# Experts' second bias moved from TensorE to VectorE, and the next item's transposes dealt out among fc2's matmuls

## What is computed

```python
logits = cos_scores + route_scores
gates = _top_k_softmax(logits, TOP_K)                       # TOP_K = 2
h = gelu(einsum('bsd,edh->bseh', x, w1) + b1, approximate=False)
expert_out = einsum('bseh,ehd->bsed', h, w2) + b2           # w1 [8,1024,512], w2 [8,512,1024]
out = einsum('bse,bsed->bsd', gates, expert_out)
...
x = x + gb * out
```

## Time and profile before

| what | value |
|---|---|
| median of 3 runs | 1535.41 us (1529.23 to 1543.14) |
| the profiled execution's own time | 1545.17 us |
| its span, first to last instruction, slowest core (core 4) | 1543.6 us |
| spans of the eight cores | 1504.7 to 1543.6 us |
| PE busy over the span | 1184.6 us, 77% |
| DVE / ACT / POOL busy | 685.8 / 490.4 / 264.4 us |
| experts' stage | about 1265 to 1543.6 us |

### The profile page before, as it was taken

The page is one execution under the profiler, slowest core; times in us unless marked ns, Lnnn a source line. Parts: engine busy times, 40 slices in busy tenths (PEclk is TensorE's granted clock), DMA queues, the critical chain, the costliest instruction groups (busy, mean ns, idle before and its releaser), DMA issues.

```text
span 1543.6 us, 24787 instructions; the slowest of 8 cores (1504.7 to 1543.6 us)
## 1 busy us (share of the span) xinstructions
PE 1184.6 (77%) x8741; PEld 697.1 (45%) x8877; DVE 685.8 (44%) x1355; ACT 490.4 (32%) x1106; POOL 264.4 (17%) x364
## 2 busy tenths in 40 slices
PE   0317898848377887777998898999999705999996
PEld 0113444424234454444765565666666402343453
DVE  0266367636363566564242533525435331223332
ACT  0003455525244465422222232222332202332242
POOL 2022111100010000011012121212211120333333
PEclk9858999979698998667999999999999956999998
DMA  9953299999868567796953737558323396888865
GB/s 162 162 115 113 68 150 152 175 128 163 132 137 75 88 118 127 146 260 172 261 143 69 178 91 143 164 83 191 98 95 111 119 365 200 165 143 156 156 124 84
DMA packets 104448, 223.12 MB, mean 145 GB/s; under 512 B 14224, under 2 KB 47152, under 8 KB 100224
## 3 DMA queue, kind: packets, MB, share of 16 engines
q0 software_dynamic: 56240, 86.70, 38.7%
q1 hardware_dynamic: 28592, 107.77, 22.9%
q10 hardware_dynamic: 19488, 26.98, 9.8%
HBM read 192.64 MB, written 117.10 MB: 201 GB/s over the span
## 4 chain that ended last, share of the span: by engine, by line
PE 55%; DMA 15%; DVE 11%; issue 7%; ACT 4%; POOL 2%; another core or an unknown queue 2%; SPq 2%; ACTq 1%; POOLq 0%; DVEq 0%
PE bank L242 22%; PE pair L242 15%; PE bank L1057 11%; DMA y<-arena 5%; DMA arena<-s_x 3%; PE bank L250 3%; DMA arena<-wmod 3%; DVE arena L590 2%; DMA lnfm<-ln_fm 2%; SPq L235 2%; ACT arena L594 2%; DMA arena<-s_xsa 1%; PE pair L566 1%; PE pair L250 1%
## 5 line engine op out<-in xcount | busy, mean ns | idle before, releaser
L242 PE MATMUL bank<-arena 128*128 128x512 bf16 (+5 forms) x1648 | 369.5, 365 | 50.3 <-ACT arena L644 22.2
L242 PE MATMUL pair<-arena 128*128 128x256 bf16 (+3 forms) x2616 | 354.9, 281 | 17.6 <-DMA arena<-wqkvT 10.7
L242 PEld LDWEIGHTS pair<-arena 128*128 128x128 bf16 x2624 | 245.8, 99 | 119.3 <-issue 29.7
L1057 PE MATMUL bank<-arena 128*128 128x512 bf16 x960 | 255.6, 382 | 6.7 <-DVE arena L1076 3.1
L242 PEld LDWEIGHTS bank<-arena 128*128 128x128 bf16 (+2 forms) x1712 | 144.8, 101 | 220.3 <-issue 108.1
L1047 ACT ACTIVATE arena<-pair,fc1b_fm 128x256 bf16<-128x256 f32 x256 | 121.3, 474 | 352.9 <-PE pair L242 349.6
L594 ACT ACTIVATE arena<-pair,arena 128x384 bf16<-128x384 f32 x256 | 146.5, 578 | 173.1 <-DVE arena L590 146.1
L250 PE MATMUL bank<-ident_bf,arena 128*128 128x128 bf16 x1056 | 96.1, 239 | 76.0 <-DVE arena L468 36.3
L1401 DVE SCALAR_TENSOR_TENSOR arena<-bank,arena,repl 128x512 f32<-128x512 f32 (+1 forms) x96 | 71.9, 749 | 161.7 <-PE bank L242 161.7
L1057 PEld LDWEIGHTS bank<-arena 128*128 128x128 bf16 x1024 | 101.0, 99 | 75.4 <-issue 10.9
L250 PEld LDWEIGHTS bank<-ident_bf,arena 128*128 128x128 bf16 x1056 | 75.4, 107 | 110.8 <-issue 95.9
(11 more groups left out here) (144 smaller groups left out, 1032.7 us busy)
## 6 DMA issues: line engine op xcount, KB each, us to landing
arena<-s_w SPq DMA_DIRECT2D x32, 1024.0 KB, 22.4
arena<-x_ext SPq DMA_DIRECT2D x34, 512.0 KB, 6.2
s_w<-w_in POOLq DMA_DIRECT2D x16, 1024.0 KB, 12.9
s_xsa<-arena ACTq DMA_DIRECT2D x4, 2084.0 KB, 37.8
arena<-s_xsa ACTq DMA_DIRECT2D x32, 260.5 KB, 5.2
s_h<-arena SPq DMA_DIRECT2D x16, 512.0 KB, 4.4
arena<-wmod POOLq DMA_DIRECT2D x16, 512.0 KB, 11.1
arena<-s_h SPq DMA_DIRECT2D x16, 512.0 KB, 11.1
```

What stands on the lines that cost most here:

```text
L242: fn = (lambda e, l=l, r=r, i=i: e.matmul(out, l, r, start=(i == 0), stop=(i == n - 1)))
L1057: T_2[mu] = run("tensor", lambda e, lt=lt, n=n, b=b: e.matmul(bf(b)[:, :], tT[mu % 4][:, ts(lt, 128)], wf2[:, m, ts(n, 512)], start=(m == ...
```

## The change

The selector and its matmuls go. Each expert's b2 row is loaded to all 128 partitions (`rs(1)` and `rs(2)` in turn, a DMA of 512 KB issued by ACT), and DVE adds it in an operation of its own, out of PSUM into `yo`, before the product with gate and gb, which now reads and writes `yo` in SBUF. `turn(n)` returns its 8 transposes and its rest; `second_mm(n, beside)` puts one transpose behind each matmul, and the rest (copy, gate, place, load) comes behind the `second_mm` of the same index k.

```diff
-    sel_bf = A.alloc("sel_bf", [8, 8 * 128], BF16)
...
-    for e_ in range(NEXP):
-        c = ident_bf[0:8, e_:e_ + 1]
-        T_sel = run("vector", lambda e, e_=e_, c=c: e.tensor_copy(
-            sel_bf[0:8, ts(e_, 128)],
-            bass.AP(c.tensor, c.offset, [[c.ap[0][0], 8], [0, 128]])))
+    T_bb = {}
+
+    def load_b2(i):
+        T_bb[i] = move("scalar", rs(1 + i % 2), bass.AP(
+            b2_in.tensor, ITEMS[i][1] * D, [[0, 128], [1, D]]),
+            esem[f"bb{i % 2}"], T_fv.get(first.get(i - 1, 0) - 1))
+
+    load_b2(0)
+    load_b2(1)
...
     def turn(n):
 
         i, j, r0 = TILES[n]
-        T_xt[n] = transposes(bb(n % 2), xs[n % 8], 8, T_xsl[n], T_xe.get(n - 2))
...
+        def one(k):
+            fn = (lambda e: e.transpose(
+                bb(n % 2)[:, ts(k, 128)], xs[n % 8][:, ts(k, 128)],
+                ident_bf[:, :]))
+            if k < 7:
+                quiet("tensor", fn, T_xsl[n], T_xe.get(n - 2), T_id)
+            else:
+                T_xt[n] = run("tensor", fn)
+
+        def evac():
+            T_xe[n] = run("scalar", lambda e: e.activation(
+                xT3[:, :, ts(j, 128)], v3(bb(n % 2), 8), AF.Copy), T_xt[n],
+                T_f1.get((i - 1, 3)))
+            ex, s = ITEMS[i][1], n % 16
+            T_gate[n] = run("vector", lambda e: e.tensor_copy(
+                gate[:, s:s + 1], xtail[n % 8][:, 1 + ex:2 + ex]), T_xsl[n],
+                T_fv.get(n - 16))
+            T_place[n] = run("gpsimd", lambda e: e.tensor_copy(
+                place[:, s:s + 1], xtail[n % 8][:, 0:1]), T_xsl[n],
+                T_add.get(n - 16))
+            if n + 8 < len(TILES):
+                load_xs(n + 8)
+        return [lambda k=k: one(k) for k in range(8)], evac
...
-    def second_mm(n):
+    def second_mm(n, beside):
...
         for nn in range(2):
-            T_f2[n] = mms(bf(b + nn)[0:w, :],
-                          [(hT3[:, m, j * 128:j * 128 + w],
-                            w23[:, ex * 4 + m, ts(nn, 512)]) for m in range(4)]
-                          + [(sel_bf[0:8, ex * 128:ex * 128 + w],
-                              b2_bf[0:8, ts(nn, 512)])],
-                          T_fv.get(n - 2), T_g[4 * i + 3], T_e2[ex], T_sel)
-            T_fv[n] = run("vector", lambda e, nn=nn: e.scalar_tensor_tensor(
-                yo[n % 5][0:w, ts(nn, 512)], bf(b + nn)[0:w, :],
-                gate[0:w, s:s + 1], rs(0)[0:w, ts(nn, 512)], ALU.mult, ALU.mult),
-                T_f2[n], T_add.get(n - 5), T_gate[n], T_gb)
+            for m in range(4):
+                fn = (lambda e, nn=nn, m=m: e.matmul(
+                    bf(b + nn)[0:w, :], hT3[:, m, j * 128:j * 128 + w],
+                    w23[:, ex * 4 + m, ts(nn, 512)], start=(m == 0),
+                    stop=(m == 3)))
+                toks = (T_fv.get(n - 2), T_g[4 * i + 3], T_e2[ex])
+                if m < 3:
+                    quiet("tensor", fn, *toks)
+                else:
+                    T_f2[n] = run("tensor", fn)
+                for f in beside[:1]:
+                    f()
+                beside = beside[1:]
+            y, cols = yo[n % 5], slice(nn * 512, nn * 512 + 512)
+            tk = run("vector", lambda e, nn=nn, y=y, cols=cols: e.tensor_tensor(
+                y[0:w, cols], bf(b + nn)[0:w, :], rs(1 + i % 2)[0:w, cols],
+                ALU.add), T_f2[n], T_add.get(n - 5), T_bb[i])
+            T_fv[n] = run("vector", lambda e, y=y, cols=cols: e.scalar_tensor_tensor(
+                y[0:w, cols], y[0:w, cols], gate[0:w, s:s + 1],
+                rs(0)[0:w, cols], ALU.mult, ALU.mult), tk, T_gate[n], T_gb)
...
     for i in range(NI):
         for m in range(4):
             first_mm(i, m)
+            if m == 1 and 1 <= i < NI - 1:
+                load_b2(i + 1)
+        fs, evs = [], []
         for n in nxt.get(i + 1, ()):
-            turn(n)
-        for n in nxt[i]:
-            second_mm(n)
+            f, ev = turn(n)
+            fs += f
+            evs.append(ev)
+        for k, n in enumerate(nxt[i]):
+            second_mm(n, fs[8 * k:8 * k + 8])
+            if k < len(evs):
+                evs[k]()
```

More of the change, by code:

```diff
@@ L1249, in build_program @@
         [f"w1{i}" for i in range(8)] + [f"w2{i}" for i in range(8)]
-        + ["b1", "gb"] + [f"xs{i}" for i in range(8)]
+        + ["b1", "gb", "bb0", "bb1"] + [f"xs{i}" for i in range(8)]
         + [f"yo{i}" for i in range(5)])}
@@ L1359, in turn @@
         i, j, r0 = TILES[n]
-        T_xt[n] = transposes(bb(n % 2), xs[n % 8], 8, T_xsl[n], T_xe.get(n - 2))
-        T_xe[n] = run("scalar", lambda e: e.activation(
-            xT3[:, :, ts(j, 128)], v3(bb(n % 2), 8), AF.Copy), T_xt[n],
-            T_f1.get((i - 1, 3)))
-        ex, s = ITEMS[i][1], n % 16
-        T_gate[n] = run("vector", lambda e: e.tensor_copy(
-            gate[:, s:s + 1], xtail[n % 8][:, 1 + ex:2 + ex]), T_xsl[n],
-            T_fv.get(n - 16))
-        T_place[n] = run("gpsimd", lambda e: e.tensor_copy(
-            place[:, s:s + 1], xtail[n % 8][:, 0:1]), T_xsl[n], T_add.get(n - 16))
-        if n + 8 < len(TILES):
-            load_xs(n + 8)
+        def one(k):
[20 more added lines that the diff above has]
+        return [lambda k=k: one(k) for k in range(8)], evac
     def first_mm(i, m):
@@ L1419, in build_program @@
     for n in nxt[0]:
-        turn(n)
+        fs, ev = turn(n)
+        for f in fs:
+            f()
+        ev()
     for i in range(NI):
```

## The result

The changed kernel takes 1599.3 us (median of 4 runs, 1598.7 to 1600.1) beside 1535.4 us for the kernel before on the same chip (median of 3 runs, 1529.2 to 1543.1): ratio 1.041, 95% interval 1.035 to 1.047. A fourth run of the kernel before, at 1553.9 us, was in the slower state into which executions on all eight cores sometimes fall, and is left out. The change makes the kernel slower by 64 us. The prediction, 1582 us, had the sign, and 17 us too little of the size.

A forecast was written before the change was run, and what follows sets the result against it. PE was taken to bound the experts' stage. Held ACT queue and smaller terms gave +33.0, half clock 10.5 and 3, total +46.5: 1535.4 to 1582 us, forecast chance 0.51, range 1548 to 1604.

The forecast's parts named there:

- The wait that decides: ACT's next copy queues behind a load awaiting POOL's cast, behind DVE's scatter: large items 23.4 us against 20.56, +19.9 over seven.
- The port: POOL's casts may each sit out a DVE multiply with two SBUF inputs: up to 0.75 us each, 10 in all; taken 0.
- PE, what comes in: Moved transposes expose two PE waits in large items: 1.15 us between fc1 and fc2, 1.4 between fc2 and next fc1.
- A transposed pair at 0.27: On PE in fc2, a matmul plus a transpose takes 0.272 us, 2.18 for a tile's eight pairs; bounds 0.216 and 0.43.
- The clock: PE falls to half clock after gaps of about 4 us: 1.5 us per large item, 1.0 in items 8 to 10; +13.5.
- Item 8: First of the small items with ACT held until POOL's casts: +4.6 us, and 1.0 for half clock.
- The b2 loads at nothing: Loads of b2 rows hide on the DMA engines in large items; 0 to 2.9 us each in items 11 to 14, taken 0.
- Item 0's gain of 2.2: At the stage's start, item 0's transposes' stretch shrinks from 3.4 to 1.15 us: -2.2.
- rival B: DVE and POOL's shared port, or adds behind b2 loads in small items, add +10 to +20: 1592 to 1602 us; chance 0.15.
- A: Rival: ACT is held but PE's clock stays up: +33, 1568 us; chance 0.19.
- C: Rival: ACT isn't held; DVE through the banks and two exposed gaps remain, large items 19.6 us: -6, 1529; chance 0.10.
- D: Rival: ACT isn't held and DVE keeps up, PE's work and two gaps count: -19, 1516 us; chance 0.05.

The follow-up runs named there:

- experiment 1: The changed kernel with loads of xs tiles 8 and up issued by SyncE's queue instead of ACT's: ratio 1.016 to the kernel before, stage 266.8 us.
- experiment 2: The changed kernel with the next item's gate copies and casts ahead of all second_mm, copies and loads left in place: stage 261.5 us against the change's 308.4.
- experiment 6: The changed kernel with the bias back as an 8-row matmul and one DVE multiply, transposes still dealt among fc2's matmuls: stage 298.6 us, large items 24.0.
- experiment 8: The changed kernel with fc2's matmuls of small items' second tile on 128 columns of weights instead of 64: stage 300.7 us.
- experiment 7: The changed kernel plus 16 throwaway matmuls in PE's gap before fc1 in items 0 to 6: stage 296.4 us, large items 23.2 or 23.3, some 24.5.
- Experiment 10: The changed kernel without item 7's four scatters, their rows missing from the output: stage 301.5 us, item 8 15.1 to 15.2.
- experiment 5: The changed kernel without b2 loads for items 2 to 15, reusing the rows of items 0 and 1: ratio 1.040 to the kernel before, stage 302.9 us.
- experiment 3: The changed kernel with the order of before (transposes, copies, casts, loads ahead of second_mm), bias still added by DVE: ratio 1.007 to the kernel before.
- experiment 4: The kernel with DVE's bias and the order of before, b2 rows of items 0 and 1 reused for items 2 to 15: ratio 0.994 to the kernel before.
- experiment 9: The kernel before with its bias matmul padded by zeros from 8 to 128 rows: ratio 0.991, large items 18.9 us.
- experiment 11: The kernel before with 128-row bias matmul, third and fourth tiles' transposes dealt among fc2, casts and gate copies ahead of second_mm: ratio 0.986, large items 17.6 us.

## Why the prediction was right in its sign and short in its size

- **The wait that decides: right.** Copy 3 was forecast 14.2 us after fc2's start; it came at 1378.45 - 1364.47 = 14.0. Experiments 1 and 2 show that it is the queue. That the number is so close is in part luck: two parts were off in opposite directions, 0.8 less and 0.6 more. DVE's half tile took 1.46 us, not 1.59 (tile 2.97, not 3.3), because an operation that depends on the one before starts 0.1 us behind it, and the next add starts 0.08 before the multiply's recorded end, where 0.06 behind it was taken; so the third tile left at 1374.90, 10.4 after the start, not 11.2. And from scatter to next copy it took 1378.45 - 1375.73 = 2.72, not 2.14. Most of that is the cast's 1.21 instead of 0.76.
- **The port, taken at nothing: 0.44 us at the cast that decides.** The cast that began at 1376.73 ended at 1377.94; a DVE multiply with both inputs in SBUF ran from 1377.16 to 1377.91. The one at 1371.30, which began with a multiply already running (from 1371.13), took 0.77. Over the eight cores a multiply began during 147 of 379 casts, and 138 of these took longer than 0.85 us, 1.21 in the median; none of the other 232 took longer than 0.77. In experiment 6 the multiply has an input in PSUM: it began during 179 casts, and none took longer than 0.77. There it is 2.28 us from scatter to next copy, not 2.72. This agrees only in part with what the Trainium skill says (SBUF — State Buffer, Who interferes with whom): the two instructions do get in each other's way, but it is the cast that is the longer one, though it began first, and the multiply keeps its 0.75. The prediction placed the cast rightly (1376.73 lies in the add from 1376.38) and overlooked the multiply that begins during it. For the seven large items that is 3 us, an estimate of 7 x 0.44; POOL's recorded times are rough.
- **PE, what comes in: right** for the two exposed gaps: PE is idle for 1.03 us before fc2 (1.15 forecast), and fc1 starts 0.14 after the copy's end (0.1 forecast).
- **A transposed pair at 0.27: right for full tiles** (1364.47 to 1366.64 is eight pairs of 0.271 in PE's timeline), **wrong for the 64-column tiles**, where it took 0.50, above even the 0.43 taken as an upper bound. That is the failed step in items 11 to 14, 1.8 us each; experiment 8 shows it by giving the forecast's 9.4.
- **The clock: right as a mechanism, mis-sized.** 1.5 us an item was taken, measured 2.1 (large items; 25.3 against 23.2 in experiment 7); and the prediction looked for it in gaps of 4 us, while stretches at 1.2 GHz also followed gaps of 1.3 us (experiment 7). In two of items 11 to 14 on core 2 it fell as well, 1.5 us each.
- **Item 8: the failed step.** The text reads that an item's first scatter waits for the adds of the item before, and then used it only to say that the chain passes over to the adds. It was not put into the sum: item 8 has four adds before it, its queue hangs on the first scatter, and the sum gave it 5.6 us instead of 12.3 (9.8 on cores 0, 3 and 5). Experiment 10 brings the item to 15.1 us, near the forecast's 14.5.
- **The b2 loads at nothing: nearly right in the large items, 5 us off over the stage** (experiment 5). The reason given, room on the DMA engines, was taken from a large item of 23.4 us. Where large items take 19.3 the loads cost 12 us of the stage (experiments 3, 4).
- **Item 7** lost 0.8 us instead of gaining 0.8. Its granted clock is 1.00 throughout. The prediction had a b2 load hold ACT's gelu for at most 0.3 us; the load of 1479.24 holds the third gelu, and without these loads the item takes 14.0 instead of 15.1 (experiment 5).
- **Item 0's gain of 2.2: counted twice.** The shorter stretch between fc1 and fc2 of item 0 (3.4 to 1.15) is already in the first of the seven periods of 20.56 and 23.4. Nothing before item 0's fourth gelu gets shorter. By its own terms the sum is +48.7, and the median after 1584.
- **Rivals.** The measured 1599.3 lies in rival B's 1592 to 1602, and B's two causes are real, but they are the smaller part of what was missing: some 5 us for the b2 loads and 3 for the port. A (clock stays up) falls by the windows above; experiment 7 comes near it, with 23.2 us where no stretch fell. C, the ACT queue not held, comes true in the large items of experiments 1 and 2 (19.2 against its 19.6), but even then the kernel is slower than before (1.016 in experiment 1), since the adds into y bind now and then and items 8 to 14 stay over 11. D never came up, as DVE's half tile is 1.46.

In sum: the table's forecasts add up to 48.2, the 46.5 of the sum without item 0's -2.2 and without the 0.5 for DVE's last tile, which lies behind the last period. Core 2's table adds up to 69.4. The 21.2 missing: item 8 6.7, the pairs of items 11 to 14 7.1 and their clock 2.9, item 7 1.6, the large items 2.8 (the clock some 4 more, the wait 1.4 less), items 9 and 10 0.1. By the medians of the cores the stage grew 64 us, and so did the times.

## What to carry to other kernels

An engine's instruction queue holds everything behind a DMA issue that waits, here 6 us of a large item of 25 (experiments 1 and 2): when a block of code is moved, ask of each DMA in it which engine issues it, what it waits for, and what stands behind it. Transposes between other matmuls are nearly free on PE, 0.056 us, if their weights have the same shape as their neighbours' (0.27 a pair against 0.50); a bias matmul of 8 rows is cheaper when padded to 128 (0.216 against 0.43). A step that removes work from the busiest engine must be read together with what it adds elsewhere: with the b2 loads beside them, the adds into y fell behind in some large items of 19.2 us (experiments 1 and 2) and in items 7 to 9 (3). Without the loads all seven large items kept 19.3, 18.9 and 17.6 us (4, 9, 11). Experiments 1 and 2 without the loads weren't run.

## What the runs showed of the hardware that wasn't expected

- A matmul of 512 columns with 8 rows between matmuls of 128 rows costs 0.43 us; padded to 128 rows 0.216 (experiment 9).
- A pair of a matmul with 64 columns of weights and a 128-column transpose takes 0.50 us; with 128 and 128 0.27 (experiment 8). Both go with weights that are loaded with their matmul, not ahead of it, where the shape of the weights changes.
- Half-clock stretches of 3.4 us and of 6.8 us came with gaps in PE of 1.3 to 3.8 us, but not every time: with the gap of 3.75 us filled, 36 of 56 large items had none behind the gap of 1.34 us.
- A POOL cast of one column takes 0.77 us, and mostly 1.21 when a DVE multiply with both inputs in SBUF begins during it; it then ended 0.03 us behind the multiply's end. A multiply with one input in PSUM didn't lengthen it (experiment 6).
